# Two attention layers on one core: the negated maxima move into the idle rows of queries and keys

## What is computed

```python
# layer 0: causal attention of x over the first 112 context rows, then layer norm
Q, K, V = relu(x @ Wq.T + bq), relu(ctx @ Wk.T + bk), relu(ctx @ Wv.T + bv)
scores = Q_ @ K_.T / 4, masked (causal, keys whose features sum to 0)
x0 = layernorm(softmax(scores) @ V_ * query_mask + x)
# layer 1
n = layernorm(x0);  q, k, v = n @ sa_wqkv
r = x0 + softmax(causal(q @ k.T / 16)) @ v @ sa_wproj + sa_bproj
k2, v2 = layernorm(ctx) @ ed_wkv;  q2 = layernorm(r) @ ed_wq
r = r + softmax(q2 @ k2.T / 16) @ v2 @ ed_wproj + ed_bproj
out = r + relu(layernorm3(x0) @ ff_w1 + ff_b1) @ ff_w2 + ff_b2
```

## Time and profile before

| | before |
|---|---|
| median of 3 runs | 367.59 us |
| profiled execution | 367.8 us |
| its span | 366.1 us |
| TensorE busy | 348.3 us (95%), 4144 matmuls |
| TensorE weight loads busy | 262.9 us (72%) |
| VectorE busy | 224.6 us (61%) |
| ScalarE busy | 170.9 us (47%) |
| GpSimd busy | 52.2 us (14%) |
| TensorE clock granted | 0.999 of full speed |

### The profile page before, as it was taken

One profiled execution on the slowest core, in us unless ns is written; L12 is line 12 of the kernel. 1 busy time (PEld: TensorE's weight loads), 2 busy tenths in 40 slices (PEclk: granted clock), 3 DMA queues, 4 the chain that ended last, 5 costly groups with the idle time before them and its releaser, 6 DMA issues.

```text
span 366.1 us, 9692 instructions
## 1 busy us (share of the span) xinstructions
PE 348.3 (95%) x4144; PEld 262.9 (72%) x4144; DVE 224.6 (61%) x563; ACT 170.9 (47%) x299; POOL 52.2 (14%) x67
## 2 busy tenths in 40 slices
PE   8988999999999999999999999999999999999996
PEld 4656788777965678876876776766987768675674
DVE  4789998436668746567945758556944464264412
ACT  2267652650664255673444062763453643614350
POOL 2023331041022010122100041130100031000000
PEclk9999999999999999999999999999999999999999
DMA  7759202000000002000000200000000000000000
GB/s 200 218 192 376 69 23 92 2 2 0 27 0 2 2 7 81 27 14 15 3 2 8 79 2 14 2 2 14 1 4 0 2 2 2 15 2 13 4 2 25
DMA packets 5300, 14.12 MB, mean 39 GB/s; under 512 B 689, under 2 KB 2982, under 8 KB 5002
## 3 DMA queue, kind: packets, MB, share of 16 engines
q1 hardware_dynamic: 4970, 13.42, 11.1%
q10 hardware_dynamic: 288, 0.09, 0.1%
HBM read 12.59 MB, written 0.92 MB: 37 GB/s over the span
## 4 chain that ended last, share of the span: by engine, by line
PE 76%; DVE 13%; DMA 5%; ACT 2%; issue 2%; SPq 1%; POOL 0%; DVEq 0%
PE ring L501 35%; PE ring L743 8%; PE acc L647 8%; PE ring L757 5%; PE ring L622 5%; DVE negmax L1031 4%; PE ring L602 4%; PE ring L596 3%; DMA xh<-in_keys 3%; PE ring L634 2%; DVE negmax L1010 2%; PE ring L666 2%; PE ring L614 2%; DMA w_qk<-in_w_qk 1%; PE ring L708 1%
## 5 line engine op out<-in xcount | busy, mean ns | idle before, releaser
L1031 DVE TENSOR_REDUCE negmax<-ring 112x2 f32<-112x750 f32 x64 | 57.0, 936 | 23.7 <-PE ring L743 23.0
L856 ACT ACTIVATE exps<-ring 125x896 f32<-125x896 f32 x48 | 41.4, 914 | 39.5 <-PE ring L757 39.2
L1248 POOL TENSOR_SCALAR_AFFINE_SELECT exps<-exps 112x896 f32<-112x896 f32 x32 | 30.8, 987 | 118.9 <-ACT exps L856 118.9
L1010 DVE TENSOR_REDUCE negmax<-ring 112x8 f32<-112x896 f32 x32 | 33.4, 1085 | 22.1 <-PE ring L602 22.0
L743 PE MATMUL ring<-k,q 32*112 32x376 f32 x256 | 38.5, 518 | 1.2 <-ACT exps L856 0.5
L647 PE MATMUL acc<-exps,v 125*17 125x112 f32 (+1 forms) x1280 | 38.9, 261 | 0.2
L647 PEld LDWEIGHTS acc<-exps,v 125*17 125x17 f32 (+1 forms) x1280 | 28.1, 97 | 12.9 <-issue 10.3
L856 ACT ACTIVATE exps<-ring,pad 112x896 f32<-112x896 f32 x32 | 30.5, 1004 | 10.7 <-PE ring L634 10.6
L501 PE MATMUL ring<-w_b,h 128*112 128x256 f32 x128 | 29.3, 382 | 0.0
L501 PEld LDWEIGHTS ring<-w_b,h 128*112 128x112 f32 x128 | 22.1, 177 | 5.8 <-issue 1.1
L501 PE MATMUL ring<-n,w_b 128*128 128x224 f32 x128 | 25.7, 357 | 0.2
(11 more groups left out here) (139 smaller groups left out, 547.2 us busy)
## 6 DMA issues: line engine op xcount, KB each, us to landing
c_nat<-in_ctx SPq DMA_DIRECT2D x4, 750.0 KB
w_b<-in_w_b SPq DMA_DIRECT2D x1, 2304.0 KB, 13.4
xk_t<-in_xk_t SPq DMA_DIRECT2D x8, 224.0 KB, 4.6
w_a<-in_w_a SPq DMA_DIRECT2D x1, 1280.0 KB, 6.0
xh<-in_keys SPq DMA_DIRECT2D x4, 224.0 KB, 4.1
x_nat<-in_x SPq DMA_DIRECT2D x4, 224.0 KB, 3.3
out<-x SPq DMA_DIRECT2D x8, 112.0 KB, 1.8
rows_sb<-in_row SPq DMA_DIRECT2D x1, 560.0 KB, 7.8
```

The costliest lines, as they stand in the source:

```text
L856: return nc.scalar.activation(exps[0:k, EXP_AT[job], :, :], o[0:k, :, 0:4 * T], ACT.Exp, bias=bias)
L1010: v_max[b].step(nc.vector.tensor_reduce(negmax[0][:, slot(g, b), 2 * m_:2 * m_ + 2, :], o[0:T, :, 0:4 * T].rearrange("p r (j t) -> p r j t ...
L1031: x_max[b].step(nc.vector.tensor_reduce(negmax[1][:, b, 2 * m_:2 * m_ + 2, i], o[0:T, :, 0:S], AX.X, ALU.max, negate=True), g, 2 * i + m_ + 1)
L1248: p_masked[b].step(nc.gpsimd.affine_select(e, e, [[0, 8], [1, T]], ALU.is_ge, 0.0, base=0, channel_multiplier=-1), g, k)
```

## The change

1. **Keys are written twice**, once for each parity `e`, with the rows of the other head set to zero by `scale`, and a one by `bias` (`one_at`) on row 16 e + c of each slice, which belongs to the other head. `kf` and `k2` get a dimension `e` of 2. In `vec` the columns for even and odd change places.
2. **The negated maxima are added to the queries** on these rows. VectorE writes the maxima of S directly at their places in `spread` (now 6 tiles of float32), TensorE transposes the tile once (M, cM), and in the new steps Q and cQ VectorE adds the transposed maxima to the idle rows of `qf` or `q2`, with two `scalar_tensor_tensor`.
3. **X and cX need no products for the maximum.** The contraction over the 32 rows holds the scores and 1 times the negated maximum. Each product has one head, 112 columns instead of 224, and there are 16 instead of 8.
4. The split of the maxima, ScalarE's copies, `ident_r`, `sel`, `maxrows` and `negmax` go.
5. `MIX` is a new merge, of 346 steps, with Q and cQ. The scratch for dynamic DMA is set to 1024.

```diff
-MIX = ("ALALNNCANDEECDCNPICWNCWDPJEWJICPDDICPJDNDIPIAJPIAAAJCJIHHJDERPCDECEDCJDCDPAIAAKAHIJNAAAPBPBEJABPJIFFIBJICPBFEFPBEBPBBBFN"
-       "DENPFBFPBEFPFEBEDCPBFBFDNKFPCDFBFBCBDCHPBDEBCKBBDCFAPBAFBFPAFDACPNBCFDCPDCPJDCBIDBBNAFAFFFJIFAAJAEIFBJFPBKFBFBIFJIPHHBPJ"
-       "BIJIPEKBEEFJHIBBBIJPIBJEFIFJIJBEPFEEFBKEFEFFBBBFBFFBHBFPBFFBFFFBBBFBFKBFFFBFFBFKFF")
+MIX = ("ALLNANADENCEDCDCNDPJDWNDCPIECJIJICWIPWJPCDPCJDNPIJIAPAIAJHDJHIRCAECCDDPCEDEPHICJDCIDIJHAJEIPAAKAJAABIBIBPABJFBJPBPEFPEBE"
+       "PPEFBENFBBPPFFKCBFBDNKBPFFFCNBFFDCNDFCBFBDABFBDBDEFCFBBCDEPPCDBPCKNAIAFBAHDPCBBDDCBCFBCADNCJCDBFFDPPBAFAFHJIAAFFAJJFIPBB"
+       "EIFBJFBFFBIFBJBIKJBKIBJBBBIFEPEEHJEIPIIJJPPIBJFIFBJIFJBEFBFEEFFFEPEHBFBFBFPFBFFBBKFBFBBBFBFFBFKBFFFFBFFBFF")
...
-        kf = [sb(f"kf{i}", [128, C, G, T]) for i in range(2)]
+        kf = [sb(f"kf{i}", [128, C, G, 2, T]) for i in range(2)]
-        k2 = [sb(f"k2_{i}", [128, G, C, SP]) for i in range(2)]
+        k2 = [sb(f"k2_{i}", [128, G, C, 2, SP]) for i in range(2)]
...
+        def spread_maxima(i):
+            return spread[i][:, :].rearrange("p (r e w) -> p r e w", e=2, w=16)[:, :, :, 0:C].rearrange("p r e c -> p r c e")
...
+            def max_rows(job, i, made):
                 o = claim(pe, job)
                 pe.wait_ge(*made)
-                for e in range(2):
-                    m = nc.tensor.matmul(o[:, 0, e * T:(e + 1) * T], spread[i][:, 128 * e:128 * e + 128], ident_r[:, :], start=e == 0, stop=True, skip_group_check=True)
-                end(m)
+                end(nc.tensor.transpose(o[:, 0, 0:T], spread[i][:, :], ident[0:T, 0:T]))
+            def shifted(bank, k, keys, queries):
                 for c in range(C):
-                    for r in range(R):
-                        rows = slice(32 * r, 32 * r + 32)
-                        nc.tensor.matmul(bank(r)[0:k, 2 * c * T:2 * (c + 1) * T], sel[rows, c:c + 1].to_broadcast([32, k]), maxrows[i][rows, :], start=c == 0, stop=False, skip_group_check=True)
+                    for e in range(2):
+                        for r in range(R):
+                            rows, j = slice(32 * r, 32 * r + 32), 2 * c + e
+                            m = nc.tensor.matmul(bank(r)[0:k, j * T:(j + 1) * T], keys(rows, c, e), queries(rows, c, e), start=j == 0, stop=True, skip_group_check=True)
+                            if j == 3 and r % 2:
+                                end(m)
...
+            def two_keys(o, s, g, bias, func):
+                for c in range(C):
+                    for e in range(2):
+                        s.step(nc.scalar.activation(kf[g % 2][:, c, :, e, :], o[:, c, 0:G * T].rearrange("p (b t) -> p b t", b=G), func, bias=bias[:, c, e:e + 1], scale=vec[:, EO + e:EO + e + 1]),
+                               g, 2 * c + e + 1)
...
                 for i in range(C):
-                    a_k2.step(nc.scalar.activation(k2[g % 2][:, b, i, :], o[:, i, 0:SP], ACT.Identity, bias=shift_k[:, i:i + 1]), g, C * b + i + 1)
+                    for e in range(2):
+                        a_k2.step(nc.scalar.activation(k2[g % 2][:, b, i, e, :], o[:, i, 0:SP], ACT.Identity, bias=shift_k[:, i, e:e + 1], scale=vec[:, EO + e:EO + e + 1]),
+                                  g, 2 * (C * b + i) + e + 1)
...
+            def less_maximum(signal_, g, k, job, q, b):
+                o = is_filled(dve, job)[:, 0, 0:T].unsqueeze(1).to_broadcast([128, C, T])
+                for e in range(2):
+                    signal_.step(nc.vector.scalar_tensor_tensor(q[:, :, b, e, :], o, vec[:, EO + 1 - e:EO + 2 - e], q[:, :, b, e, :], ALU.mult, ALU.add), g, 2 * k + e - 1)
...
-    nc = bacc.Bacc("TRN2", target_bir_lowering=False, num_devices=1)
+    nc = bacc.Bacc("TRN2", target_bir_lowering=False, num_devices=1, dynamic_dma_scratch_size=1024)
```

More of the change, by code:

```diff
@@ L266, in build @@
         exps = sb("exps", [CH, NE, 2, 4 * T])
-        negmax = [sb(f"negmax{i}", [T, (2 - i) * G, R, 4]) for i in range(2)]
-        spread = [sb(f"spread{i}", [T, 2 * 130], F32R) for i in range(3)]
-        maxrows = [sb(f"maxrows{i}", [128, 2 * T], F32R) for i in range(6)]
+        spread = [sb(f"spread{i}", [T, 128]) for i in range(6)]
         acc_sb = [sb(f"acc_sb{i}", [128, 4, T]) for i in range(3)]
@@ L624, in self_max_rows @@
             def self_max_rows(g, l, b):
-                max_rows(("M", g, l, b), v_spread[b].at(g, 2 * l + 2))
+                max_rows(("M", g, l, b), slot(g, b), v_max[b].at(g, 4) if l else v_seen[b].done(g))
             def self_shifted(g, l, b):
                 bank = quad(("X", g, l, b))
-                pe.wait_ge(*a_m[b].at(g, l + 1))
-                minus_max(bank, slot(g, b), T)
-                for c in range(C):
-                    for r in range(R):
-                        rows = slice(32 * r, 32 * r + 32)
-                        m = nc.tensor.matmul(bank(r)[0:T, 2 * c * T:2 * (c + 1) * T], kf[g % 2][rows, c, b, :],
-                                             qf[g % 2][rows, c, b, :, :].rearrange("p e t -> p (e t)"), start=False, stop=True, skip_group_check=True)
-                        if c == C - 1 and r % 2:
-                            end(m)
+                pe.wait_ge(*v_less[b].at(g, 2 * l + 2))
@@ L639, in add_values @@
+                shifted(bank, T, lambda rows, c, e: kf[g % 2][rows, c, b, e, :], lambda rows, c, e: qf[g % 2][rows, c, b, e, :])
             def add_values(s, vals, job, opens):
@@ L747, in cross_max_rows @@
             def cross_max_rows(g, b):
-                max_rows(("cM", g, b), x_spread[b].done(g))
+                max_rows(("cM", g, b), 4 + b, x_max[b].done(g))
             def cross_shifted(g, b, ch):
                 bank = quad(("cX", g, b, ch))
-                pe.wait_ge(*c_m[b].done(g))
-                minus_max(bank, 4 + b, CH)
-                for c in range(C):
-                    for r in range(R):
-                        rows = slice(32 * r, 32 * r + 32)
-                        m = nc.tensor.matmul(bank(r)[0:CH, 2 * c * T:2 * (c + 1) * T], k2[g % 2][rows, b, c, ch * CH:(ch + 1) * CH],
-                                             q2[g % 2][rows, c, b, :, :].rearrange("p e t -> p (e t)"), start=False, stop=True, skip_group_check=True)
-                        if c == C - 1 and r % 2:
-                            end(m)
+                pe.wait_ge(*x_less[b].done(g))
+                shifted(bank, CH, lambda rows, c, e: k2[g % 2][rows, b, c, e, ch * CH:(ch + 1) * CH], lambda rows, c, e: q2[g % 2][rows, c, b, e, :])
             def cross_sum(g, b, ch):
```

132 lines of the change are left out of this document (54 added, 78 removed).

## The result

The changed kernel takes 370.4 us (median of 7 runs, 369.8 to 372.3), the kernel before 367.7 on the same chip. The ratio is 1.008, with a 95% interval of 1.005 to 1.011. Forecast were 358.6 us and a range of 349.0 to 366.5, so the time lies outside the range and on the slower side. The profiled execution took 371.5 us, with a span of 369.6 and a mean granted clock of 0.991 (before: 0.999).

What follows compares the result with a forecast made beforehand. The prediction took TensorE, busy for 95% of the span, to bound the kernel. From the profiled 367.8 us, minus 11.0 plus 2.0 gave 358.8, and 358.6 us for the median, with a range of 349 to 366.5.

Steps and rivals of the forecast that it cites:

- 11.0 us won on TensorE: TensorE's sum: 8.8 us from 40 shifted score steps plus 2.2 us from M and cM as one transpose.
- 1 us for the additions that do meet a busy VectorE: Path from maxima to exponentials: 1 us added for additions standing in VectorE's queue behind a maximum.
- 1 us for the longer hold of k2: ScalarE: k2 holds its pair of banks for four writes, 1.1 us longer in 8 places; 1 us added.
- The bound: Whole kernel: TensorE busy 95%, 76% of the last chain; time taken from its steps should show.
- The shifted step, 0.22 us, 8.8 in all: X and cX on TensorE: each of 40 steps 0.22 us shorter from start to start, 8.8 us; range 6.4 to 19.1.
- the shortest-step end, 6.4: X and cX: low end of the saving, 0.16 us a step against the shortest old step, times 40.
- The remark on serial weight loads: X and cX: loads one behind the other would cost 0.75 us more a step; the trace was taken to disagree.
- M, 2.2 us: M and cM on TensorE: one transpose instead of two products saves 2.2 us, ends 0 and 4.5.
- the two other pairs cover that unless VectorE is late with both: k2's banks: the 1.1 us longer hold in 8 places is covered by the two other pairs of banks.
- The merge alone is worth nothing by this count: Order of steps: counted over 24 paths to X, old and new orders each fall short by about 4 us.
- bank emptying takes most of it back: Rival, VectorE and ScalarE: one in four of 27 us added delays TensorE, 7 of 11 us go, 363.8 us; chance 0.20.
- The slower rival: M to X: additions wait behind a 0.94 us maximum in 24 paths, 379 us; at two thirds, 372; slower's chance 0.09.

Runs made afterwards that it cites:

- keys once: Changed method with keys written for parity 0 only and used for both parities: 369.8 us in the old order, 371.1 us in the new order.
- small additions: Changed method in the old order, additions cut to one query column of each 112: 381.7 us; with keys written once as well, 363.5 us.
- fillers: Changed kernel with 14 extra float32 products, results unused, in three places at the start where TensorE idles: 370.2 us, ratio 1.008.
- additions aside: Changed method with additions written to a scratch tile and X not waiting for them: 374.1 us in the new order, 382.4 us in the old.
- the old method in the new order: Kernel before with the changed kernel's merge, Q and cQ taken out and cM20 moved behind O301: 418.9 us, ratio 1.138.

## Why the prediction was wrong

Forecast were 11.0 us won on TensorE and 2.0 lost by the added work; the step that failed is the second, "1 us for the additions that do meet a busy VectorE, and 1 us for the longer hold of k2": in the old order this work costs 21.9 us, and 6.9 are left of it with the new one. The 11.0 were too large besides; the runs give 4.2 (5.0 less 0.8).

The runs, as a ledger (us; clock: the granted clock of the runs, lowest to highest):

```
kernel                                              median   change   clock
before                                               367.7            0.99 to 1.00
without the subtraction, old order                   360.6    -7.1    0.995 to 1.00
+ products split in two                              362.7    +2.1    0.994 to 1.00
+ new path, M as one transpose, keys once,
  additions of one column                            363.5    +0.8    0.994 to 1.00
+ additions in full                                  369.8    +6.3    0.986 to 0.995
+ second copy of the keys                            385.4   +15.7    0.967 to 0.982
new order (the changed kernel)                       370.4   -15.0    0.986 to 0.994
```

Point by point, by the prediction's steps.

- **The bound.** Right: TensorE's time counts in full, 7.3 of 7.2 us and 27.5 of 28.0.
- **The shifted step, 0.22 us, 8.8 in all.** The mechanism was right, the size off: 0.17 and 0.10 clean, 5.1 us, and as runs 7.1 - 2.1 = 5.0 (7.1 from the ledger's medians; against the kernel before on its own chip it is 7.3). I compared a mean of old steps, 1.26, which holds waits, with a clean step. Clean against clean was the shortest-step end, 6.4, less the longer cross step. The remark on serial weight loads stays refuted: 16 x 0.02 + 24 x 0.10 us for the split, not 0.75 a step.
- **M, 2.2 us.** Start to start 7.7 became 6.5 with the waits, and 3.7 in the old order with keys once and small additions. There the rest of the new path took it back: it is inside the +0.8.
- **"I add 1 us for the additions that do meet a busy VectorE".** This term failed: in the old order their length costs 6.3 us with keys once and 3.8 with keys twice. X's wait for them is not the main reason: without it 0.2 us were gained behind the start of the old order, and 0.3 in the new one. That leaves VectorE's queue, by elimination; in the start, the two were not separated.
- **"1 us for the longer hold of k2"; "the two other pairs cover that unless VectorE is late with both".** This is the step that failed most: the second copies cost 15.7 us in the old order with the rest of the method, and 11.4 alone. Priced was only the hold of k2's pair. Not priced was what stands behind the copies in ScalarE's queue: exponentials, which hold another pair, and the copies of k0 and k1, which TensorE's next S needs. In the new order the copies cost nothing that keys once would give back.
- **"The merge alone is worth nothing by this count".** It is worth 15.0 us. The count looked at the 24 paths from M to X and not at who empties which bank when. The new order has almost no waits for key copies. It pays for that in other steps: the sum of O and cO is 12.5 to 13.1 us in every run of the old order with full maxima, and 15.7 to 16.0 in every such run of the changed method in the new one; cT is 6.6 to 6.8 against 8.0 to 8.2.
- **The rival "bank emptying takes most of it back"** named the cause; it assumed that one in four of 27 us delays TensorE. Together the additions' length and the copies cost 21.9 us in the old order, four in five. The Trainium skill, TensorEngine Tiling (Array Packing), section PSUM Bottleneck, says that tiling speeds up TensorE but not the emptying of PSUM; this case agrees (11.4 us for the copies alone), and adds that an engine with 47 to 49% busy time can be that limit.
- **The slower rival** (VectorE's queue in the path, 372 to 379) had the sign and not the mechanism.

So the sum in hindsight: 5.0 us won by the products, 0.8 lost by the path, 21.9 by the added work, 15.0 given back by the order: 367.7 - 5.0 + 0.8 + 21.9 - 15.0 = 370.4. Against the forecast's terms, 3.8 of the missing 11.8 us are the step's size (5.0 instead of 8.8), 3.0 are M and the path (0.8 lost instead of 2.2 won), and 4.9 are the added work net of the order (6.9 instead of 2.0).

Two things stay open. A part of the 15.7 and the 15.0 us goes with the clock, since the runs without waits had 1.00 and those with the most waits 0.967 to 0.982; within the latter, 382.6 us at 0.982 and 386.5 at 0.967 belong together, so at full clock the old order would be some 378 by that slope, an estimate. Keys once there would be some 368.5 in the same way (a line through its ten runs), and the changed kernel with fillers took 369.1 at 1.0. That would leave some 9 us for the copies and as much for the order. Whether the clock fell because of these waits was not tried. And the changed kernel is still 7 us above the 363.5 of the old order without the added work. By the sums 4.9 us of the difference between these two traces are in O, cO and cT, which every run in the new order has, with keys once and additions aside too. No run takes the additions' length away in the new order, so its share, and the cause of the longer O and cT, stay open. No version that leaves nothing of the work out beat the kernel before.

## What to carry to other kernels

Price an instruction that is added to an emptying engine by what stands behind it in that engine's queue and by which banks those hold, not by the engine's share of busy time: 15 us on a half idle ScalarE cost 11 in the old order, and in the new order, which has other work in those places, nothing that could be measured. When a change comes with a new hand-made order, the two can't be judged apart: undo each part in the old order, where the others stay fixed, and compare traces step by step, since a run's edit or a low clock can cost time in the start that has nothing to do with the question. And compare clean steps with clean steps; ask of what is removed whether it was the expensive part (0.18 us of fp32r products against 0.69 of f32 ones).

## What the runs showed of the hardware

Eight products of 224 columns on 32-row slices cost 0.18 us a step between fp32r tiles, one of them broadcast, and 0.69 between f32 tiles. Splitting f32 products of 224 columns in two of 112 costs 0.02 us in a step of 16 with 112 keys, 0.10 with 125. An addition from PSUM to SBUF takes 214 ns for 2 elements a partition and 445 for 224. And the mean granted clock was about 1.00 where TensorE waited little, and also in the changed kernel with 27.5 us of products added, while runs with more waits had stretches at 1.2 GHz and lower means, down to 0.953 in the profile of the old method in the new order, where TensorE was busy for 87% of the span.
